# A Mamba-like block and an FP4 feed-forward: the partial state from rounded halves, delta and x's rest on GpSimd

## The reference, cut to what matters

```python
xz = x @ W_in;  x_proj, z = split(xz)              # 512 + 512
x_conv = silu(causal_conv4(x_proj) + conv_b)
ssm = x_conv @ W_xproj                             # 1 + 16 + 16 columns
delta = softplus(ssm[..., 0]); Bm, Cm = ssm[..., 1:17], ssm[..., 17:]
h_mean = einsum('bld,bln->bdn', x_conv, delta[..., None] * Bm) / L
y = (einsum('bdn,bln->bld', h_mean, Cm) + D * x_conv) * silu(z)
x = layernorm(x + y @ W_out)
# feed-forward: x, the weights and h are rounded to FP4 in blocks of 16 with a scale each
h = silu(q(x) @ q(w_gate).T) * (q(x) @ q(w_up).T)
x = layernorm(x + q(h) @ q(w_down).T)
```

## Time and profile before

| | |
|---|---|
| median of 3 runs | 1904.05 us (1903.38 to 1904.14) |
| profiled execution | 1903.5 us, its span 1901.5 us |
| busy | PE 1823.6 (96%), PEld 1518.4 (80%), DVE 1571.0 (83%), ACT 1265.9 (67%), POOL 1096.1 (58%) |
| DMA | 190.60 MB, mean 100 GB/s |
| granted TensorE clock | 0.989 of 2.4 GHz over the span |

### The profile page before, as it was taken

The page is one execution under the profiler, slowest core; times in us unless marked ns, Lnnn a source line. Parts: engine busy times, 40 slices in busy tenths (PEclk is TensorE's granted clock), DMA queues, the critical chain, the costliest instruction groups (busy, mean ns, idle before and its releaser), DMA issues. The chain is left out here.

```text
span 1901.5 us, 34283 instructions
## 1 busy us (share of the span) xinstructions
PE 1823.6 (96%) x10180; PEld 1518.4 (80%) x10180; DVE 1571.0 (83%) x3549; ACT 1265.9 (67%) x2617; POOL 1096.1 (58%) x1760
## 2 busy tenths in 40 slices
PE   6897999999999999999999999999999999899986
PEld 5665788888888888888888888888888888777775
DVE  5645788888888888988888888888889888888885
ACT  6776667677766767776676777667677766544443
POOL 3434465666666666666656666666566565555553
PEclk9899999999999999999999999999999999999998
DMA  5235232333332233333223332332333232122200
GB/s 175 95 107 170 92 104 93 108 103 117 100 112 103 94 107 104 119 98 114 100 97 105 107 115 98 114 102 98 106 106 112 102 99 94 63 81 70 76 31 17
DMA packets 120309, 190.60 MB, mean 100 GB/s; under 512 B 15040, under 2 KB 49728, under 8 KB 120128
## 3 DMA queue, kind: packets, MB, share of 16 engines
q1 hardware_dynamic: 120128, 188.42, 29.8%
HBM read 104.48 MB, written 83.89 MB: 99 GB/s over the span
## 5 line engine op out<-in xcount | busy, mean ns | idle before, releaser
L535 PE MATMUL pgu<-wgu_hi,xqT 128*128 128x512 f32 (+1 forms) x1536 | 416.4, 379 | 16.3 <-issue 15.0
L535 PEld LDWEIGHTS pgu<-wgu_hi,xqT 128*128 128x128 f32 x1536 | 279.7, 189 | 67.9 <-issue 18.8
L535 PE MATMUL pd<-wd_hi,hqT 128*128 128x256 f32 x1536 | 289.4, 287 | 5.2 <-DVE scratch L1225 2.0
L535 PEld LDWEIGHTS pd<-wd_hi,hqT 128*128 128x128 f32 x1536 | 237.6, 189 | 9.1 <-issue 4.7
L414 POOL TENSOR_SCALAR rs<-ssq 128x1 f32<-128x1 f32 x256 | 73.4, 287 | 286.5 <-issue 251.1
L1109 DVE SCALAR_TENSOR_TENSOR acc<-xps,cw,acc 128x512 f32<-128x512 f32 x256 | 200.3, 782 | 34.0 <-POOL acc L453 29.2
L535 PE MATMUL pgu<-wgu_lo,xqT 128*128 128x512 f32 (+1 forms) x768 | 227.4, 377 | 0.0
L1024 DVE SCALAR_TENSOR_TENSOR scratch<-scratch 128x256 f32<-128x256 f32 (+2 forms) x258 | 171.5, 665 | 61.7 <-ACT scratch L903 60.1
L805 ACT ACTIVATE scratch<-scratch,sum 128x256 f32<-128x256 f32 x256 | 130.2, 508 | 119.8 <-DVE scratch L1171 109.7
L611 PE MATMUL pd<-wout,g 128*128 128x256 f32 x864 | 204.0, 379 | 0.0
L416 POOL TENSOR_TENSOR rs<-rs,nhalf 128x1 f32<-128x1 f32 x256 | 178.6, 698 | 21.3
(11 more groups left out here) (142 smaller groups left out, 4447.6 us busy)
## 6 DMA issues: line engine op xcount, KB each, us to landing
sz_hbm<-szs SPq DMA_DIRECT2D x128, 256.0 KB, 2.0
xc_hbm<-xcs SPq DMA_DIRECT2D x128, 256.0 KB, 2.0
early<-xc_hbm SPq DMA_DIRECT2D x128, 256.0 KB, 2.7
early<-sz_hbm SPq DMA_DIRECT2D x128, 256.0 KB, 3.0
xin<-in_x_t_dram SPq DMA_DIRECT2D x32, 512.0 KB, 4.7
xres<-in_L_attn_x_dram SPq DMA_DIRECT2D x128, 128.0 KB, 2.3
out_dram<-scratch SPq DMA_DIRECT2D x128, 128.0 KB, 1.7
early<-in_L_attn_W_in_dram SPq DMA_DIRECT2D x2, 512.0 KB, 4.7
```

The costliest lines, as they stand in the source:

```text
L535: mm = pe.matmul(bank, lhsT, rhs, start=(m == 0), stop=(m == len(pairs) - 1))
```

## The change

- **partial_state** of the second group and of all from the fifth on takes F32R operands: `xct` holds the rounded x_conv and its rest (`conv_rest`, VectorE, from PSUM; one buffer each), `dBr` holds dB rounded three times, 16 zero columns, its own rest in 16 columns, and zeros up to 128 columns. Eight matmuls of 128 columns by 512 in place of four in full fp32. In the steady part it is called in step 1, before state_projection, which goes behind z_product there; add_state moves to step 1 too. For the other early groups the full x_conv lies in memory used later.
- **hacc, hcat, ctr, ccat** have 80 rows in place of 48; GpSimd makes one more copy of C.
- **scaled_b** moves from step 1 to step 0, behind h_round and conv_rest; from group 6 on delta is made by GpSimd in two instructions behind the copies of C. dB takes three instructions.
- **x's rest** (`split_input`) moves from VectorE to GpSimd, one half each in steps 2 and 3, before the products of h; ScalarE's part moves from step 2 to step 1.
- **transposed_c** stands behind down_projection and writes to `pc`; x_product waits for `conv_rest` of the step before and no longer for c_copy.

The diff, cut to its core:

```diff
+        xct = sb("xct", [P, 2, TPS, DI], F32R)
+        dBr = sb("dBr", [P, TPS, P], F32R)
+        dBx = sb("dBx", [P, TPS, NS])
+        def split_state(k):
+            return k == 1 or k >= LAG - 1
         def c_bank(g_):
-            return pd if g_ <= LAG else pa
+            return pd if g_ <= LAG else pc
 # gpsimd
+            def split_input(g_, k):
+                at_least(pool, z_pe, 4 * (g_ - 1))
+                pool.wait_ge(xt_h, 2 * g_ + k + 1)
+                pool.tensor_tensor(xt_lo[:, g_ % 2, k, :], xin[:, k, :], xt_hi[:, g_ % 2, k, :].bitcast(F32),
+                                   ALU.subtract).then_inc(xt_l, 1)
                         layer_norm(to, ssq1_done, r1_ready, rs1_eps, rs1_done, nm1_done, sum1, ssq1, rs1, nm1)
+                    if g_ > LAG and j >= 2 and exists(g_ + 1, NSUP):
+                        split_input(g_ + 1, j - 2)
...
                         pool.tensor_copy(c2[:, :, 0, :].bitcast(F32R), c_in)
+                        pool.tensor_copy(ccat[:, :, HL:HR].bitcast(F32R), c_in)
...
+                        if g_ > LAG:
+                            pool.tensor_scalar(dpos[:, :], ssm[:, (g_ - 1) % 2, :, 0], 0.0, 0.0, ALU.max, ALU.add)\
+                                .then_inc(dpos_ready, 1)
+                            pool.wait_ge(dpos_ready, g_ - LAG)
+                            pool.wait_ge(sp_link, 3 * g_)
+                            at_least(pool, dB_ready, g_ - 1)
+                            pool.tensor_tensor(delta[:, :], dpos[:, :], sp[:, 2, :], ALU.add).then_inc(d_ready, 1)
 # tensor
+                if split_state(n - 1):
+                    pe.wait_ge(xct_rest, split_blocks(4 * n))
+                    for t in range(TPS):
+                        pe.matmul(pc[:, :], dBr[:, t, :], xct[:, 0, t, :], start=(t == 0), stop=False)
+                        mm = pe.matmul(pc[:, :], dBr[:, t, :], xct[:, 1, t, :], start=False, stop=(t == TPS - 1))
...
-                    if j == 2 and tail:
+                    if j == 1 and tail:
                         partial_state(g_, v, w)
-                    if j != 2 and exists(v):
+                    if j != 1 and exists(v):
                         state_projection(j, jb, g_, v, w)
                         transposed_conv(g_, jb, u, v)
...
-                    if j == 2 and exists(v):
+                    if j == 1 and exists(v):
                         state_projection(j, jb, g_, v, w)
                         transposed_conv(g_, jb, u, v)
+                    if exists(td):
+                        down_projection(g_, to, td)
                     if j == 3 and tail:
                         transposed_c(g_, v)
-                    if exists(td):
-                        down_projection(g_, to, td)
 # vector
                     def scaled_b():
-                        dve.wait_ge(sp_link, 3 * g_)
-                        dve.scalar_tensor_tensor(delta[:, :], ssm[:, (g_ - 1) % 2, :, 0], 0.0, sp[:, 2, :],
-                                                 ALU.max, ALU.add).then_inc(d_ready, 1)
+                        if g_ <= LAG:
+                            ...
                         dve.wait_ge(d_ready, g_)
...
+                        dve.tensor_tensor(dBr[:, :, 0:H3].rearrange("p t (a n) -> p t a n", a=3), *thrice,
+                                          ALU.mult).then_inc(dB_high, 1)
+                        dve.tensor_tensor(dBx[:, :, :], b_in, delta[:, :].unsqueeze(2).broadcast_to([P, TPS, NS]),
+                                          ALU.mult).then_inc(dB_exact, 1)
+                        dve.wait_ge(dB_high, n)
+                        dve.wait_ge(dB_exact, n)
+                        dve.tensor_tensor(dBr[:, :, HL:HR], dBx[:, :, :], dBr[:, :, 0:NS],
+                                          ALU.subtract).then_inc(dB_ready, 1)
+                    def conv_rest():
+                        if not split_state(v // TPS):
+                            return
+                        view = conv_bank(g_).rearrange("p (t n) -> p t n", t=TPS)
+                        dve.wait_ge(xct_copied, v + 1)
+                        dve.tensor_tensor(xct[:, 1, :, jb * P:(jb + 1) * P], view,
+                                          xct[:, 0, :, jb * P:(jb + 1) * P], ALU.subtract).then_inc(xct_rest, 1)
...
                     if exists(tg):
                         h_round()
-                    if j == 2 and exists(v):
+                    if j == 1 and exists(v):
                         add_projection()
-                    if j == 1 and tail:
+                    if exists(v):
+                        conv_rest()
+                    if j == 0 and tail:
                         scaled_b()
                     if j == 3 and s == 0 and tail:
                         mean_state()
-                    if j == 2 and exists(g_ + 1, NSUP):
-                        split_input(g_ + 1)
```

More of the change, by code:

```diff
@@ L315, in out_bank, with split_blocks, whole_conv @@
             return pa if g_ > NSUP else pd
+        def split_state(k):
+            return k == 1 or k >= LAG - 1
+        def split_blocks(n):
+            return min(max(n - 4, 0), 4) + max(n - 4 * (LAG - 1), 0)
+        def whole_conv(k):
+            place = scratch[:, 4 * GW:4 * GW + TPS * DI] if k == LAG - 2 else early[:, :]
+            return place.rearrange("p (t n) -> p t n", t=TPS)
         def conv_bank(g_):
@@ L486, in body @@
                             .then_inc(cc_ready, 1)
+                        if g_ > LAG:
[5 more added lines that the diff above has]
+                            pool.tensor_tensor(delta[:, :], dpos[:, :], sp[:, 2, :], ALU.add).then_inc(d_ready, 1)
+                    if j == 2 and g_ <= LAG:
+                        for k in range(KM):
+                            split_input(g_ + 1, k)
                     weight_products(u)
+            for k in range(KM):
+                split_input(0, k)
             walk(body)
@@ L556, in gate_and_up, with transposed_free @@
                 mm.then_inc(gu_pe, 1)
+            def transposed_free(n):
+                if n > 0 and split_state((n - 1) // TPS):
+                    pe.wait_ge(xct_rest, split_blocks(n))
+                else:
+                    at_least(pe, xct_copied, n)
             def x_product(j, g_, u, v):
@@ L620, in partial_state @@
                 at_least(pe, yd_done, capped(w + 1, NT))
-                for t in range(TPS):
-                    mm = pe.matmul(pc[0:H3, :], dB[:, t, :], xct[:, (n - 1) % 2, t, :],
-                                   start=(t == 0), stop=(t == TPS - 1))
+                if split_state(n - 1):
[3 more added lines that the diff above has]
+                        mm = pe.matmul(pc[:, :], dBr[:, t, :], xct[:, 1, t, :], start=False, stop=(t == TPS - 1))
+                else:
+                    for t in range(TPS):
+                        mm = pe.matmul(pc[0:H3, :], dB[:, t, :], whole_conv(n - 1)[:, t, :],
+                                       start=(t == 0), stop=(t == TPS - 1))
                 mm.then_inc(h_pe, 1)
@@ L716, in body @@
                             partial_state(g_ - 1, v, w)
+                        if j == 1 and g_ == LAG:
+                            partial_state(g_, v, w)
                         if exists(v):
@@ L858, in conv_copy @@
                         act.wait_ge(xct_pe, v + 1)
-                        act.activation(xct[:, (g_ - (1 if j == 0 else 0)) % 2, :, jb * P:(jb + 1) * P],
-                                       conv_bank(g_).rearrange("p (t n) -> p t n", t=TPS), ACT.Copy)\
+                        if v == 0:
+                            act.wait_ge(win_l, 2)
+                        if v == 4 * (LAG - 2):
+                            act.wait_ge(wq_ready, 1)
+                        place = xct[:, 0, :, :] if split_state(v // TPS) else whole_conv(v // TPS)
+                        act.activation(place[:, :, jb * P:(jb + 1) * P], conv_bank(g_).rearrange("p (t n) -> p t n", t=TPS), ACT.Copy)\
                             .then_inc(xct_copied, 1)
@@ new lines, in scaled_b @@
+                        thrice = (b_in.unsqueeze(2).broadcast_to([P, TPS, 3, NS]),
+                                  delta[:, :].unsqueeze(2).unsqueeze(3).broadcast_to([P, TPS, 3, NS]))
+                        if not split_state(g_ - 1):
+                            dve.tensor_tensor(dB[:, :, :].rearrange("p t (a n) -> p t a n", a=3), *thrice,
+                                              ALU.mult).then_inc(dB_ready, 1)
+                            return
+                        n = split_blocks(4 * g_) // TPS
@@ L1282, in body @@
                         tap(2)
-                        if j == 3:
-                            split_input(g_ + 1)
-                            if LAG - 1 <= g_:
-                                add_state(g_)
+                        if j == 3 and g_ == LAG - 1:
+                            add_state(g_)
                         if p2:
@@ L1292, in body @@
                             add_state(g_ - 1)
```

(6 more changed lines are left out.)

75 lines of the change are left out of this document (40 added, 35 removed).

## The result

The changed kernel takes **2004.47 us** (2003.47 to 2005.25), the kernel before in the same job 1903.81 (1903.38 to 1904.14): ratio 1.0528 [1.0515, 1.0541]. Forecast were 1944 us, 1892 to 1988: the sign was right, the size was not. The profiled execution's span is 2002.3 us against 1901.5, +100.8.

The account below looks back on a forecast made before the run. TensorE, busy throughout the steady part, was taken to bound the kernel. 27 x (1.07 + 0.25) = 36 us, plus 5 for mean_state and 0 for the first groups, gave about +40 on 1904.05: 1944 us, range 1892 to 1988.

Parts of the forecast that it names:

- What decides, and the chain of waits: Steps 0 to 1: VectorE waits 2.7 us for GpSimd's delta, lags 4.64, idles TensorE 2.3 at skip; step 1 17.57.
- the floor: TensorE's own list for one steady group with rounded state matmuls: 53.63 us, 1.70 less than before.
- The state matmuls at 0.23 in the sum: Partial state in step 1: eight rounded matmuls at 0.23 us each, 1.87 us, replacing 3.57 in step 2.
- at the edge: TensorE's 2.3 us gap: in the earlier profile clock fell to 0.59 after 2.38 us, stayed 1.00 after 2.23.
- The clock below 1.00: Listed sign of being wrong: TensorE's granted clock below 1.00 in the steady part.
- Ordinary groups as a whole: Steady groups 6 to 32: each longer by 1.07 us, plus 0.25 for x's rest; 36 us over 27 groups.
- x's rest; 0.39 for 0.25: x's rest moved to GpSimd in steps 2 and 3: collisions with VectorE cost 0.25 us a group (0 to 0.4).
- mean_state, "+0.7": Step 0 after mean_state in every fourth group: starts 2.4 us late, +0.7 in seven groups, +5 us in all (0 to 13).
- Groups 0 to 5, "I take 0": First groups: two partial states save 1.7 each, GpSimd has 2.6 us more six times; -3 to +3, taken as 0.
- Faster: Rival: VectorE's lag never reaches TensorE, group 53.63 us, total 1855 us; chance 0.18.
- Clock: Rival: TensorE's clock falls in step 1's new gap, +1.3 us in 27 groups, total 1979 us; chance 0.15.
- Slow matmuls: Rival: rounded state matmuls run at 0.45 us each, 1.1 more in 27 groups, total 1974 us; chance 0.05.

Follow-up runs that it names:

- g3: g2 with state_projection and the transposes of conv behind down_projection in step 1: 1882.1 us, 0.9884 of the kernel before.
- g5: g4 with skip() and scaled_b ahead of the taps in step 1 of group 5: 1864.8 us, 0.9794 of the kernel before.
- f2: Changed kernel with step 1's state matmuls behind z_product, then down_projection, state_projection; delta and dB on VectorE in step 1 behind the taps: 1966.5 us.
- g1: Changed kernel with delta and the three dB instructions on VectorE in step 1, behind the taps, ahead of x_round: 1928.2 us, 1.0123 of the kernel before.
- g2: g1 with x's rest back on VectorE, ahead of h_round in steps 2 and 3: 1893.2 us, 0.9941 of the kernel before.
- g4: g3 with mean_state ahead of conv_rest in step 3 and hacc's clearing replaced by a copying first add_state: 1868.7 us, 0.9812 of the kernel before.
- e3: Changed kernel with x's rest back on VectorE behind step 2's work, first groups as before; delta stays on GpSimd: 2000.8 us.
- e4: Changed kernel with twenty matmuls of zeros filling TensorE's gap before step 1's state matmuls, groups 6 to 32: 1983.7 us.
- e1: Changed kernel with delta again one VectorE instruction at the end of step 0, before the dB products: 1944.3 us, 1.0213 of the kernel before.

## Why the prediction was right in sign and wrong in size

*What decides, and the chain of waits: right.* VectorE 2.63 us idle for delta (2.7 forecast), TensorE 2.66 for skip (2.3), step 1 without the half clock = lag + 13.1 (12.93); lag 4.86 (4.64). The saving on the matmuls is real too: step 2 is 12.74 (12.80), and g3 reaches the floor. (Eight matmuls of 0.23 are 1.84 us, not 1.87; g5 shows 1.95.)

*The state matmuls at 0.23 in the sum: wrong, 1.02 us a group.* This is the step that failed in step 1. It took the gap's length, "at the edge" of two rows of the first groups, and left the clock to a rival at 0.15. In 17 of 18 ordinary groups the clock fell and the matmuls ran 0.43 apart. With the lag's own bounds (3.9 to 5.7) more than half of the range of gaps (lag - 2.3) lay above the 2.38 of the row that fell; since the lag moved the gap up as well, the two belonged in one case. And two rows, one event each, could not show an edge: group 7 has 2.67 us and no fall, f2 falls behind 1.75. The clock below 1.00 was one of the prediction's own signs of being wrong.

*Ordinary groups as a whole:* +2.88 against 1.32: clock 1.02, lag 0.22, constant 0.17, and 0.14 from steps 0, 2 and 3 (x's rest; 0.39 for 0.25; g1 against g2 has 0.58 less there without it). 18 such groups are 28 us of the miss.

*mean_state, "+0.7": measured 5.08, of which 2.88 is the ordinary loss.* The second step that failed: I added the old 1.81 us of mean_state to the lag of an undisturbed step 3. mean_state starts behind h_round's longer second half (x's rest), and behind conv_rest, which puts its hcat beside the products of h (499 ns to 1239 in the mean; 1.53 us in g3 too, where x's rest is gone). So VectorE starts step 0 5.13 us late (2.4 forecast), and that step takes 16.80 us, with a gap on TensorE: 17.57 in the three groups where the clock fell there, 16.0 in the three where it fell in step 1. g4 shows the part of mean_state's place and clearing (56.31 to 54.09), g1 against g2 that of x's rest (58.75 to 56.43, of which 0.87 in every group). 6 x (5.08 - 1.32 - 0.7) = 18 us of the miss.

*Groups 0 to 5, "I take 0": +10.8 at the start of group 7, against 1.3 for group 6 in the sum.* The third term, put at nothing. 2.8 is x's rest on GpSimd (e3); g4 to g5 takes 4.5 away, the wait for dB in group 5 with its half clock; g5 keeps 2.1. The 1.4 between e3 and g4 was not taken apart, nor was g5's 2.1.

The three, and 4 more from groups 31 and 32, are the 60 us between 1944 and 2004.

*The rivals.* "Faster" did not hold in the changed kernel: it needed a lag of 2.3 at most, and g2 to g5, which have 1.06, are what it described. "Clock" was a true part, at 1.02 us a group for 1.3. "Slow matmuls" is refuted: in group 7, e4 and g5 the state matmuls run at 0.23, and 0.43 was the clock.

## What to carry to other kernels

Before an operation is moved, look at what stands ahead of it in its new queue and at what the neighbouring engine runs at that moment: as the changed kernel has them, with delta on GpSimd and dB behind the products of h, step 1 takes 18.98 us; with both on VectorE behind the taps of step 1 it takes 15.76 (g1). Of the 3.2 us 1.02 are the clock. On a bounding engine a new gap has two prices, its length and the slow clock behind it; if the gap's range reaches rows behind which the clock fell, put both in the sum. A long queue has work that covers a wait: find out what each candidate waits for itself before it is moved there.

## What the runs showed of the hardware

In the changed kernel a gap of 2.66 us in a TensorE list that is full otherwise was followed by about 3.1 us of work at 1.2 GHz in 17 of 18 ordinary groups. The length of a gap alone did not decide. The clock stayed at 1.00 behind 2.67 us in group 7; behind 2.33 to 2.38 us (e3) it fell in 5 of 17 ordinary groups (step 1 18.6 to 18.7 us, 17.6 in the others); behind 1.75 to 2.06 us (f2) in 8 of 18; behind 1.37 to 1.42 us in step 0 of the groups with mean_state in 4 of 6 (g3) and in 2 of 6 (g2); behind 1.25 to 1.66 us in the ordinary groups of e1 in none of 18. What else decides was not tested.

A VectorE write of 80x512 from one SBUF input to SBUF (hcat) also waits for GpSimd: it takes 417 ns where it starts first (g4) and 1.53 us where the product of h started 0.17 us before it (g3), though it has no second input. The Trainium skill (SBUF — State Buffer, Who interferes with whom) counts tensor_scalar among the operations that can take the shared ports in a two-port mode; the runs agree.
